# A two-layer graph network on one core: GpSimd waits for each slot's gathers to land before it issues the next slot's

## The reference

```python
h = jnp.maximum(_layernorm(x), 0.0)
# layer one: weighted mean of W0-projected source rows over the edges of each target
hw = h @ W + b
agg = segment_sum(edge_w[:, None] * hw[edge_src], edge_dst, 6250)
deg = segment_sum(edge_w, edge_dst, 6250)
x = x + relu(agg / (deg[:, None] + 1e-06))
h = jnp.maximum(_layernorm(x), 0.0)
# layer two: a message for each edge, summed over the edges of each target
messages = gelu(concat([h[src], edge_attr]) @ W_msg + b_msg)
agg = segment_sum(messages, dst, 6250)
x = x + gelu(((1.0 + eps) * h + agg) @ W_upd + b_upd)
```

## Time and profile before

| | |
|---|---|
| timed, three runs | median 2670.86 us (2669.74 to 2680.39) |
| the profiled execution: span from first to last instruction | 4082.0 us |
| mean granted TensorE clock in it | 0.844 |
| busy: TensorE 2950.6, VectorE 2089.7, GpSimd 1835.1, ScalarE 1607.4 us | |

### The profile page before, as it was taken

How to read it: one execution, slowest core, us unless ns; L and a number is a source line. 1 busy time by engine, 2 the same in 40 slices (tenths; PEclk the granted TensorE clock), 3 DMA queues, 4 the chain that set the end, 5 groups by cost and what they waited for, 6 DMA issues and landing times.

```text
span 4082.0 us, 72599 instructions
## 1 busy us (share of the span) xinstructions
PE 2950.6 (72%) x22325; PEld 2600.4 (64%) x22326; DVE 2089.7 (51%) x4376; ACT 1607.4 (39%) x5144; POOL 1835.1 (45%) x1911
## 2 busy tenths in 40 slices
PE   2776766665665666576788788778878878878887
PEld 2666665554554555565677677677767767767777
DVE  8444445544544554544455455555545545555554
ACT  2343333433433443334344444444434444444443
POOL 2333344334434434424455545545545554554552
PEclk9888787877777777787888888888888888888888
DMA  4000000000000000002333333333333333333332
GB/s 92 14 12 14 13 16 16 13 13 15 14 12 15 15 13 14 15 14 66 75 84 85 81 81 84 87 79 83 88 76 86 83 81 81 84 87 78 85 88 52
DMA packets 473123, 214.39 MB, mean 53 GB/s; under 512 B 264996, under 2 KB 442024, under 8 KB 473076
## 3 DMA queue, kind: packets, MB, share of 16 engines
q1 hardware_dynamic: 412404, 151.55, 14.2%
q0 software_dynamic: 60672, 62.25, 9.2%
HBM read 208.14 MB, written 5.51 MB: 52 GB/s over the span
## 4 chain that ended last, share of the span: by engine, by line
PE 41%; issue 11%; another core or an unknown queue 1%; DVE 1%; DVEq 0%; ACT 0%; ACTq 0%
PE ps L918 28%; PE ps L1123 6%; PE ps L988 5%; PE ps L1112 2%; DVE sel L1451 0%; PE ps L1070 0%; DVE rows L1455 0%; DVEq L1464 0%; PE ps L1017 0%; ACT eT L844 0%; DVE sums_sb L1472 0%; DVE parts L1219 0%; DVE room L1654 0%; ACT dw L652 0%
## 5 line engine op out<-in xcount | busy, mean ns | idle before, releaser
L629 POOL DMA_INDIRECT rows<-p_table,idx x1176 | 1109.4, 943 | 1065.6 <-ACT idx L660 736.0
L918 PE MATMUL ps<-parts,pick_all 128*128 128x448 f32 x5488 | 1241.0, 379 | 63.5 <-issue 59.9
L629 POOL DMA_INDIRECT rows<-h_table,idx x720 | 709.5, 985 | 1062.1 <-ACT room L760 857.7
L918 PEld LDWEIGHTS ps<-parts,pick_all 128*128 128x128 f32 x5488 | 1046.3, 195 | 193.6 <-issue 109.4
L947 PE MATMUL ps<-adj,h_sb 128*64 128x160 f32 (+1 forms) x4802 | 503.4, 342 | 516.4 <-issue 469.9
L947 PEld LDWEIGHTS ps<-adj,h_sb 128*64 128x64 f32 x4802 | 404.4, 170 | 608.8 <-issue 551.9
L1451 DVE TENSOR_TENSOR sel<-ps,mask 128x896 f32<-128x896 f32 x196 | 213.5, 1089 | 761.4 <-remote 541.9
L1388 DVE TENSOR_SCALAR hot_p<-iota_p,scal 128x256 fp32r<-128x256 f32 (+1 forms) x848 | 309.4, 365 | 410.9 <-PE ps L928 321.6
L928 PE MATMUL ps<-hot_c,hot_p 128*128 128x125 f32 (+1 forms) x2336 | 456.3, 302 | 87.6 <-issue 72.4
L721 ACT COPY adj<-ps 128x500 f32<-128x500 f32 (+1 forms) x848 | 389.8, 524 | 203.0 <-PE ps L928 126.5
L928 PEld LDWEIGHTS ps<-hot_c,hot_p 128*128 128x128 f32 x2336 | 377.4, 207 | 110.5 <-issue 86.5
(11 more groups left out here) (181 smaller groups left out, 2975.9 us busy)
## 6 DMA issues: line engine op xcount, KB each, us to landing
src_all<-keys SPq DMA_DIRECT2D x196, 448.0 KB
ea<-in_edge_attr_dram SPq DMA_DIRECT2D x196, 256.0 KB
rows<-p_table,idx POOLq DMA_INDIRECT x1176
rows<-h_table,idx POOLq DMA_INDIRECT x720
x_sb<-in_x_dram SPq DMA_DIRECT2D x6, 224.0 KB, 3.5
h_table<-h_sb SPq DMA_DIRECT2D x6, 224.0 KB
p_table<-h_sb SPq DMA_DIRECT2D x6, 224.0 KB
out_dram<-h_sb SPq DMA_DIRECT2D x6, 224.0 KB
```

What stands on the lines that cost most here:

```text
L629: nc.gpsimd.indirect_dma_start(out=rows[:, s, j, 0:D], out_offset=None, in_=table[:, :], in_offset=bass.IndirectOffsetOnAxis(ap=idx[:, s, ...
L918: last = nc.tensor.matmul(to, hot[:, k, t * P:(t + 1) * P], parts[:, part, k, :, :].rearrange("p a d -> p (a d)"), start=(k == 0 and part ...
```

## The change

After the gathers of a slot in layer one, GpSimd waits until the slot's gather semaphore has reached the value that stands for this turn's gathers, then increments a semaphore that no one waits for (`s_passed`). The value is `z.gathered(b) * 16 + 16 * z.JH` with `b = turn - 1`. Layer two passes no value and is as before.

```diff
-                def gathers(turn, tiles):
+                def gathers(turn, tiles, landed=None):
                     for s in range(SLOTS):
                         pool.wait_ge(s_const, CONSTS)
                         pool.wait_ge(s_idx[s], turn)
...
                             ).then_inc(s_gat[s], 16)
+                        if landed is not None:
+                            pool.wait_ge(s_gat[s], landed)
+                            pool.sem_inc(s_passed, 1)
 
                 if layer == 0:
                     for z in ZONES:
                         with pool.Fori(z.first + 1, z.end + 1) as turn:
-                            gathers(turn, range(z.JA, J))
+                            gathers(turn, range(z.JA, J), z.gathered(turn - 1) * 16 + 16 * z.JH)
```

## The result

The changed kernel takes 3041.5 us (3039.7 to 3046.7, four runs) beside 2675.6 us for the kernel before (2669.7 to 2680.8, four runs): a ratio of 1.138, 95% interval 1.135 to 1.141. The runs of the kernel before fall into two groups some 10 us apart, which is why its median lies 5 us above the one in the table of before. The forecast had the direction and the mechanism (GpSimd stops behind each slot until the rows have landed), but priced a turn of the loop too low.

What follows compares the result with a forecast made beforehand. The prediction took GpSimd's gather issue as the bound in the timed run. It summed 212 us around the loops, 1259 for layer one's 48 turns with waits and 1480 for layer two to 2951 us, range 2855 to 3040.

Steps and rivals of the forecast that it cites:

- 17.1 us of idleness: GpSimd's stop after each 16-gather burst in layer one's profile, until ScalarE scaled a slot's rows; taken as absent when timed.
- holes: TensorE's adjacency products run singly, 1.4 to 2.9 us apart, in layer one: 15.8 us a body, ascribed to the profiled execution.
- faster: Rival: gathers in flight cause TensorE's holes, so breaks between slots let it run; 66 us come back, 2605; chance 0.04.
- GpSimd is the bound there: In the timed run GpSimd's work fills 2582 of 2671 us, leaving 89 us of slack in both loops together.
- 20 to 21 us: TensorE's assumed length for a 12-gather turn in layer one, beside 15 us of GpSimd's work.
- 1480: Layer two's term in us: its floor of 1470 plus 10 of the 89 us of slack.
- 1.95 us: Price of one added wait in layer one: landing 1.74 plus restart 0.5 less the usual gap of 0.3.
- 22.8 us, or 27.8 us: Layer one's turn of 12 or 16 gathers with four waits, set by GpSimd; 1259 us over 48 turns.
- 212 + 2370: GpSimd's forced time around the loops plus 1896 gathers at 1.25 us: 2582, 97% of the timed 2671.
- 989: Most us layer one's loop could take in the timed run for its 48 turns after the first.
- 2.6 us a wait: Upper bound for one wait, allowing a longer first gather after a stop: turns 25.4 and 30.4 us, total 3076.
- The change could look free: Only next-slot gathers queue behind a wait, and ScalarE needs them one body later, no sooner than a slot's own landing.

Runs made afterwards that it cites:

- before_again: The kernel before, unedited, profiled once more: span 2667.5 us, timed 2669.3 us (one run).
- one_less: The kernel before, without any wait, leaving out one gather per slot in layer one: 2662.6 us, ratio 0.9973.
- layer2_less: The kernel before, without waits, leaving out one gather per slot in layer two: 2668.8 us, ratio 1.001.
- last_slot_only: The changed kernel with only the wait behind each turn's last slot kept (49 in place of 196): 2755.0 us, ratio 1.031.
- zone2_only: The changed kernel with the waits kept in the 33 bodies of 16 gathers only: 2945.8 us, ratio 1.101.
- one_more: The kernel before, without any wait, each layer-one slot issuing one extra gather whose rows are not used: 2850.1 us, ratio 1.065.
- layer2_waits: The same waits placed in layer two instead of layer one (196 waits): 3096.3 us, ratio 1.159.
- issued_only: The changed kernel, but each wait is for GpSimd's own completion of the slot's last gather, not for the rows: 2751.2 us, ratio 1.029.
- one_behind: The changed kernel, but each wait is for the slot before (147 waits, never slot 3): 2670.4 us, ratio 0.999.

## Why the prediction was short of the time

**Reading the profile.** Right: that the 17.1 us of idleness is not there in a timed run, that a gather's 1.25 us is, and that GpSimd's 1896 gathers leave almost no room. before_again shows all three. The holes' cause stays open: no later profile had them, so nothing could be tried on them, and the rival that lived on them (faster) has no ground here. The instruction queues carried no more in the execution that has them: the pages of before and before_again both list the same 47 packets there for the whole execution (25 on q8, 22 on q14), beside 270 holes in 1080 us of the first.

**"GpSimd is the bound there."** Not quite: one_less shows that the other engines give a late body 21.2 us, and layer2_less that TensorE gives one of layer two 30.5, and GpSimd's work lies 1.0 and 0.5 us below. In the early turns it is 17.2 against 15.2, and the 20 to 21 us I gave them were TensorE's busy time in the disturbed profile at a clock of 0.85. For the forecast this hardly mattered, since its loop rests on the turn after; it did for last_slot_only, zone2_only, one_more and layer2_waits.

**The sum.** Span 3044.9 against 2951, by its own terms:

| term | forecast | measured | |
|---|---|---|---|
| before the second turn | 29.3 + 59.0 | 98.6 | +10.3 |
| 48 turns | 1259 | 1343.1 | +84.1 |
| between the layers | 70.6 | 52.1 | -18.5 |
| layer two | 1480 | 1496.2 | +16.2 |
| end | 53 | 55.0 | +2.0 |

The step that failed is the second line, the price of a turn: "1.95 us" a wait, 1.25 us a gather, and so "22.8 us, or 27.8 us" a turn. The turns are 24.0 and 29.9 us, which makes 84 us in 48 turns, nearly the whole miss; the other lines together come to 10.

Half of the late turn's 2.1 us is the stops: 2.80 + 2.40 + 2.37 + 2.40 = 10.0 us, where 4 x 2.25 = 9.0 was expected. The landing itself was priced rightly. Rows 9 have 1.74 us with VectorE's 0.26 us of restart in it, so 1.48 for the landing, and the gap of the full wait less that of issued_only is 1.5. What was too small is GpSimd's restart: 0.87 us behind its own gather (issued_only) in place of the 0.74 of rows 10. And the seam's extra 0.4 us was not in the sum at all.

The other half is the gathers. They are recorded with 1.00 us on average in the late turns in place of 0.94, 16 times, and the 12 gaps between them are 0.32 us in place of 0.30. A part of this could be read before the change: rows 2 give layer one's gathers 985 ns and layer two's 943, and the sum took layer two's for both. In before_again the late turns' gathers are 0.96 us without any wait, so the stops add 0.04. The upper bound had allowed for a longer gather; the central value dropped it on the strength of a row of layer two, where it indeed doesn't occur. Why it does in layer one is open.

The first line of the table is a slip in my own sum: the first turn's 12 gathers (15 us) stand in "212 + 2370" but were forgotten when the 1259 us of 48 turns took the place of layer one's gathers. With them the forecast would have been 2966 and the same range's upper end 3055, above the measured time, while the turns were still priced too low. The slip also put the loop's bound before at 989 instead of 974; measured 964.

Layer two's 1480 was 16 us short because its body is TensorE's 30.5 us, not GpSimd's 30.0 with a little slack. That the other lines nearly cancel is luck.

**The range.** Its upper end of 3040 was tighter than my own case of 2.6 us a wait (3076). The measured cost of a wait, all in, is (1343 - 885) / 192 = 2.4 us, inside the bounds of 1.45 to 2.6. Cutting the range short of a bound that the text had worked out was a second mistake.

**"The change could look free."** Right that nothing but the next slots' gathers stands behind the wait, and right that ScalarE then comes to each slot before or as its gathers land: from 700 to 1400 us it waits for gathers for 350 us.

## What to carry to other kernels

Before idle time in a profile is counted as cover, compare the span with the timed median; where they differ, add up what the engine must do in the timed run, and profile again if that is possible. A self-imposed wait costs an issuing engine its landing and its restart (here 1.5 and 0.57 us), and only where the engine's work plus its waits exceeds the length the body has from the others: price both, and take the larger. If a landing has to be respected, wait for it one slot later, where it was already past here for 67 of 68 gathers.

## What the runs showed of the hardware that was not expected

A wait of GpSimd on its own completion of a gather (no landing) makes the next gap 0.87 us in place of 0.30, and 1.32 at the seam of two turns, though without a wait that gap is 0.30 too. Waits on events already past leave it at 0.30 (one_behind, ratio 0.999). The cause of either is not shown.

A gather in layer one is recorded with 0.96 us on average without waits (before_again) and 1.00 with them (after), but layer two's stay at 0.94 us, with and without waits.

One execution of this kernel, profiled, took 4082 us, at a mean clock of 0.84. In it TensorE ran single products 1.4 to 2.9 us apart while gathers were being issued. Eleven later profiles, of it, the changed kernel and the variants, recorded in the same way, did not show it.

The same closing products of TensorE ran at a granted clock of 0.50 in some profiles and 1.00 in others, after the same work, which moves the end of the execution by 12 us.
